# The linear-attention block of a decoder: bias products on 96 rows, a gate by tanh with one reciprocal per head, the residual added on VectorE

## What is computed

```
q, k, v = heads(x @ Wq.T + bq), heads(x @ Wk.T + bk), heads(x @ Wv.T + bv)
g = jax.nn.sigmoid(heads(x @ Wg.T + bg))
q, k = jax.nn.elu(apply_rope(q)) + 1.0, jax.nn.elu(apply_rope(k)) + 1.0
def step(carry, inp):                       # over the two chunks of a sequence
    S, Z = carry
    qi, ki, vi, gi = inp
    S = S + jnp.einsum('bhtd,bhte->bhde', ki, vi)
    Z = Z + ki.sum(axis=2)
    num = jnp.einsum('bhtd,bhde->bhte', qi, S)
    den = jnp.einsum('bhtd,bhd->bht', qi, Z)[..., None] + 1e-06
    return ((S, Z), gi * num / den)
...
x = _layernorm(x + (out @ Wo.T + bo))
```

## Time and profile before

| | |
|---|---|
| median of three runs | 1009.85 us |
| the profiled execution, its own time | 1009.48 us |
| its span, first to last instruction | 1007.7 us |
| mean granted TensorE clock | 0.994 |
| PE busy | 963.4 us (96%) |
| DVE busy | 642.2 us (64%) |
| ACT busy | 444.5 us (44%) |
| POOL busy | 312.0 us (31%) |

### The profile page before, as it was taken

The page is one execution under the profiler, slowest core; times in us unless marked ns, Lnnn a source line. Parts: engine busy times, 40 slices in busy tenths (PEclk is TensorE's granted clock), DMA queues, the critical chain, the costliest instruction groups (busy, mean ns, idle before and its releaser), DMA issues.

```text
span 1007.7 us, 18735 instructions
## 1 busy us (share of the span) xinstructions
PE 963.4 (96%) x6131; PEld 757.6 (75%) x6131; DVE 642.2 (64%) x1466; ACT 444.5 (44%) x870; POOL 312.0 (31%) x514
## 2 busy tenths in 40 slices
PE   7999999999999999999999989998999998999994
PEld 5788886688888888888887745567787775888883
DVE  3776777656555555555557567768777865555555
ACT  4777786422233222323222333325777784333331
POOL 1133123344444444444445130110000106344430
PEclk9999999999999999999999999999999999999998
DMA  8000000255433333333332000011111120554401
GB/s 282 19 17 18 2 2 1 65 169 179 144 127 115 110 112 110 116 110 110 110 113 88 0 10 1 1 34 38 30 33 36 34 67 21 126 154 109 111 20 42
DMA packets 37356, 75.20 MB, mean 75 GB/s; under 512 B 7116, under 2 KB 18360, under 8 KB 37154
## 3 DMA queue, kind: packets, MB, share of 16 engines
q1 hardware_dynamic: 37006, 74.18, 25.5%
q0 software_dynamic: 288, 0.23, 0.2%
HBM read 67.21 MB, written 2.40 MB: 69 GB/s over the span
## 4 chain that ended last, share of the span: by engine, by line
PE 87%; DVE 7%; issue 2%; ACT 1%; POOL 1%; DMA 0%; SPq 0%; POOLq 0%; DVEq 0%; ACTq 0%
PE ps L1053 34%; PE ps L1079 17%; PE ps L424 5%; PE ps L674 3%; PE ps L519 3%; PE ps L431 3%; PE ps L913 2%; PE ps L511 2%; PE ps L550 2%; PE ps L791 1%; PE ps L846 1%; PE ps L841 1%; DVE ps L1748 1%; PE ps L810 1%; PE ps L888 1%
## 5 line engine op out<-in xcount | busy, mean ns | idle before, releaser
L1053 PE MATMUL ps<-shared 128*128 128x512 f32 x1560 | 377.8, 391 | 1.2 <-POOL shared L2096 0.7
L1053 PEld LDWEIGHTS ps<-shared 128*128 128x128 f32 x1560 | 292.9, 188 | 65.4 <-issue 4.9
L1489 ACT ACTIVATE shared<-pT 128x512 fp32r<-128x512 f32 x130 | 82.2, 632 | 286.5 <-DVE pT L1909 286.5
L2109 POOL CAST shared<-wraw 128x512 fp32r<-128x512 f32 (+1 forms) x130 | 92.2, 709 | 293.1 <-PE ps L1079 279.5
L1912 DVE TENSOR_TENSOR al<-pT,shared 128x512 fp32r<-128x512 f32 x130 | 118.8, 914 | 90.8 <-ACT shared L1489 90.8
L1901 DVE TENSOR_TENSOR e<-e,ps 128x512 f32<-128x512 f32 x130 | 89.3, 687 | 122.1 <-PE ps L1053 117.8
L1079 PE MATMUL ps<-shared 128*128 128x512 f32 x520 | 160.3, 389 | 0.4 <-DVE al L1912 0.4
L2111 POOL TENSOR_TENSOR shared<-wraw,shared 128x512 fp32r<-128x512 f32 (+1 forms) x130 | 132.1, 1017 | 10.4
L1079 PEld LDWEIGHTS ps<-shared 128*128 128x128 f32 x520 | 97.5, 188 | 21.4 <-DVE al L1912 1.3
L1483 ACT ACTIVATE e<-ps 128x512 f32<-128x512 f32 x130 | 77.7, 597 | 73.4 <-PE ps L1053 73.4
L1909 DVE TENSOR_TENSOR pT<-e,kbd 128x512 f32<-128x512 f32 x130 | 99.9, 769 | 7.1
(11 more groups left out here) (230 smaller groups left out, 1397.8 us busy)
## 6 DMA issues: line engine op xcount, KB each, us to landing
kbd<-combine_C SPq DMA_DIRECT2D x46, 512.0 KB
wraw<-in_C_w SPq DMA_DIRECT2D x48, 384.0 KB, 8.6
kbd<-combine_F SPq DMA_DIRECT2D x15, 512.0 KB
wraw<-in_F_w SPq DMA_DIRECT2D x17, 384.0 KB, 6.9
kbd<-kbd SPq DMA_DIRECT2D x96, 32.0 KB, 1.9
kT<-kbd SPq DMA_DIRECT2D x48, 32.0 KB, 1.8
c_ctx_t<-in_ctx_t SPq DMA_DIRECT2D x1, 1024.0 KB, 9.1
out<-c_x_rows SPq DMA_DIRECT2D x2, 512.0 KB, 3.0
```

The costliest lines, as they stand in the source:

```text
L1053: mm = pe.matmul(GU[t][s], w[u][:, (c * 2 + s) * P:(c * 2 + s + 1) * P], xx[:, c, t * HALF:(t + 1) * HALF], start=(i == 0), stop=(i == 5))
L1489: act.activation(ah[t][:, :], a2[t], ACT.Copy).then_inc(S("ah"), 1)
L2109: pool.tensor_copy(wh[u][:, lo:hi], wraw[k][:, lo:hi]).then_inc(S("m_wh"), 1)
```

## The change

Four things are changed, all in block D:

1. The bias rows are 96 instead of 33, of which 94 are zeros, in the three kinds of bias product (L672 twice and L725 once per sequence); the DMA and the GpSimd cast of these rows grow with them.
2. The gate is sigmoid(g) = (1 + tanh(g/2)) / 2. `gates` calls Tanh where it called Exp, and `linear_out` takes the reciprocal of 2 (den + 1e-6), 16 numbers per token, and multiplies it by 1 + tanh; before, it took the reciprocal of (1 + exp(-g)) (den + 1e-6), 256 numbers per token.
3. The residual is added by VectorE when it reads the output projection from PSUM; the product with the identity (L726) and ScalarE's `linear_z` go.
4. `numerators` waits for `D_an` first, and for the first two sequences issues three products of `pe_keep_pace` before its other waits.

```diff
-        braw = arena[0:33, filled["DE"]:filled["DE"] + 5 * D + P]
+        braw = arena[0:96, filled["DE"]:filled["DE"] + 5 * D + P]
...
-                    pe.matmul(ps[:, n, :], ones33[:, :], brow[:, n * HALF:(n + 1) * HALF], start=True, stop=False)
+                    pe.matmul(ps[:, n, :], ones96[:, :], brow[:, n * HALF:(n + 1) * HALF], start=True, stop=False)
...
             def numerators(b):
 
+                if b > 0:
+                    pe.wait_ge(S("D_an"), b)
+                if b < 2:
+                    pe_keep_pace(pe, 5, 3)
                 pe.wait_ge(S("D_qf"), b + 1)
                 pe.wait_ge(S("D_gm"), b + 1)
-                if b > 0:
-                    pe.wait_ge(S("D_an"), b)
...
-                pe.matmul(y_, ones33[:, :], brow[:, 2 * HALF:], start=True, stop=False)
-                pe.matmul(y_, ident[:, :], X[:, b, :], start=False, stop=False)
+                pe.matmul(y_, ones96[:, :], brow[:, 2 * HALF:], start=True, stop=False)
...
-                    act.wait_ge(S("D_div"), 3 * (b - 2) + 2)
+                    act.wait_ge(S("D_div"), 3 * (b - 2) + 3)
...
-                act.activation(eg[b % 2][:, :], ps[:, 1, 0:D], ACT.Exp, scale=-1.0).then_inc(S("D_eg"), 1)
+                act.activation(eg[b % 2][:, :], ps[:, 1, 0:D], ACT.Tanh, scale=0.5).then_inc(S("D_eg"), 1)
...
-            def linear_z(b):
-
-                act.wait_ge(S("y"), nb("D", b + 1))
-                if b >= 2:
-                    act.wait_ge(S("xn"), nb("D", b - 1))
-                act.activation(z[b % 2][:, :], ps[:, 6, 0:D], ACT.Copy).then_inc(S("z"), 1)
...
-                dve.tensor_scalar(den2, num[:, :, :, DH0], 1e-6, None, ALU.add).then_inc(S("D_div"), 1)
+                dve.tensor_scalar(den2, num[:, :, :, DH0], 1e-6, 2.0, ALU.add, ALU.mult).then_inc(S("D_div"), 1)
                 dve.wait_ge(S("D_div"), 3 * b + 1)
+                dve.reciprocal(dinv[:, :], den[:, :]).then_inc(S("D_div"), 1)
+                dve.wait_ge(S("D_div"), 3 * b + 2)
                 dve.wait_ge(S("D_eg"), b + 1)
-                dve.scalar_tensor_tensor(d2[:, :].rearrange("p (h w) -> p h w", w=DH0),
+                dve.scalar_tensor_tensor(r2[:, :].rearrange("p (h w) -> p h w", w=DH0),
                                          eg[b % 2][:, :].rearrange("p (h w) -> p h w", w=DH0), 1.0,
-                                         bc(den[:, :], 2, DH0), ALU.add, ALU.mult).then_inc(S("D_div"), 1)
-                dve.wait_ge(S("D_div"), 3 * b + 2)
-                dve.reciprocal(r2[:, :], d2[:, :]).then_inc(S("D_div"), 1)
+                                         bc(dinv[:, :], 2, DH0), ALU.add, ALU.mult).then_inc(S("D_div"), 1)
...
+            def linear_residual(b):
+
+                dve.wait_ge(S("y"), nb("D", b + 1))
+                dve.tensor_tensor(z[b % 2][:, :], ps[:, 6, 0:D], X[:, b, :], ALU.add).then_inc(S("z"), 1)
+                dve_stats(dve, "D", b, b % 2)
...
                 if at(t - 4) is not None:
-                    dve_stats(dve, "D", t - 4, t % 2)
+                    linear_residual(t - 4)
...
-            pool.tensor_copy(rows33, braw[:, :]).then_inc(S("brow"), 1)
+            pool.tensor_copy(rows96, braw[:, :]).then_inc(S("brow"), 1)
...
-    d["D_brow"] = np.zeros((33, 5 * D + P), np.float32)
+    d["D_brow"] = np.zeros((96, 5 * D + P), np.float32)
```

More of the change, by code:

```diff
@@ L162, in build @@
         gm = oT[:, 0, :].rearrange("p (n c k) -> p n c k", n=2, c=C)
-        rows33 = shared[2][0:33, 0:5 * D + P]
-        brow = shared[2][0:33, 0:5 * D]
-        ones33 = shared[2][0:33, 5 * D:5 * D + P]
+        rows96 = shared[2][0:96, 0:5 * D + P]
+        brow = shared[2][0:96, 0:5 * D]
+        ones96 = shared[2][0:96, 5 * D:5 * D + P]
         den = sb("den", [P, 16])
-        d2 = sb("d2", [P, D])
+        dinv = sb("dinv", [P, 16])
         r2 = sb("r2", [P, D])
@@ L1378, in act_linear_cross @@
             for t in range(B + 1):
-                if at(t - 4) is not None:
-                    linear_z(t - 4)
                 if at(t - 3) is not None:
@@ L1400, in act_linear_cross @@
                 ep, es, ev, ef, el = (at(t - B - n) for n in range(5))
-                if t == B + 1:
-                    linear_z(t - 4)
                 for k in range(STEPS):
@@ L1421, in act_linear_cross @@
                         masks(es, k + 1)
-                    if k == 3 and do is not None:
-                        linear_z(do)
                     if k == 3 and ep is not None:
@@ L1677, in linear_out @@
                 num = ps[:, 4:6, 0:D].rearrange("p r (m w) -> p r m w", w=VW)
-                two = [x[:, :].rearrange("p (r m w) -> p r m w", r=2, w=DH0) for x in (eg[b % 2], d2, r2, an)]
+                two = [x[:, :].rearrange("p (r m w) -> p r m w", r=2, w=DH0) for x in (r2, an)]
                 den2 = den[:, :].rearrange("p (r m) -> p r m", r=2)
-                dve.tensor_scalar(den2, num[:, :, :, DH0], 1e-6, None, ALU.add).then_inc(S("D_div"), 1)
+                dve.tensor_scalar(den2, num[:, :, :, DH0], 1e-6, 2.0, ALU.add, ALU.mult).then_inc(S("D_div"), 1)
                 dve.wait_ge(S("D_div"), 3 * b + 1)
+                dve.reciprocal(dinv[:, :], den[:, :]).then_inc(S("D_div"), 1)
+                dve.wait_ge(S("D_div"), 3 * b + 2)
                 dve.wait_ge(S("D_eg"), b + 1)
-                dve.scalar_tensor_tensor(d2[:, :].rearrange("p (h w) -> p h w", w=DH0),
+                dve.scalar_tensor_tensor(r2[:, :].rearrange("p (h w) -> p h w", w=DH0),
                                          eg[b % 2][:, :].rearrange("p (h w) -> p h w", w=DH0), 1.0,
-                                         bc(den[:, :], 2, DH0), ALU.add, ALU.mult).then_inc(S("D_div"), 1)
-                dve.wait_ge(S("D_div"), 3 * b + 2)
-                dve.reciprocal(r2[:, :], d2[:, :]).then_inc(S("D_div"), 1)
+                                         bc(dinv[:, :], 2, DH0), ALU.add, ALU.mult).then_inc(S("D_div"), 1)
                 dve.wait_ge(S("D_div"), 3 * b + 3)
@@ L1690, in linear_out @@
                     dve.wait_ge(S("D_atr"), b)
-                dve.tensor_tensor(two[3], num[:, :, :, 0:DH0], two[2], ALU.mult).then_inc(S("D_an"), 1)
+                dve.tensor_tensor(two[1], num[:, :, :, 0:DH0], two[0], ALU.mult).then_inc(S("D_an"), 1)
+            def linear_residual(b):
+                dve.wait_ge(S("y"), nb("D", b + 1))
+                dve.tensor_tensor(z[b % 2][:, :], ps[:, 6, 0:D], X[:, b, :], ALU.add).then_inc(S("z"), 1)
+                dve_stats(dve, "D", b, b % 2)
             def residual(b):
@@ L1813, in dve_linear_cross @@
                     if k == 4 and do is not None:
-                        dve_stats(dve, "D", do, do % 2)
+                        linear_residual(do)
                     if k == 4 and ep is not None:
```

## The result

The changed kernel took 1002.92 us in the median of five runs (1001.23 to 1003.81). The kernel before, run beside it, now has 1012.53 in the median of its five (1009.58 to 1013.3). The ratio is 0.9912, 95% interval 0.9894 to 0.993: faster by some 9 us, where 12 were forecast, and 0.9 us above the upper end of the range. Profiled execution against profiled execution, it is 1002.89 against 1009.48, or 6.6 us for a sum of 11.95.

The account below looks back on a forecast made before the run. TensorE was taken to bound the middle of block D, VectorE the head of block E. Terms -10.0 - 1.55 + 0.34 - 0.73 = -11.95 us took the profiled 1009.48 to 997.5, 997.9 for the median; range 995.5 to 1002.

Parts of the forecast that it names:

- first sequences: Start of block D: numerators(0) at about 600.85 us instead of 602.72, 1.87 us earlier, with project(0)'s and project(1)'s gains included.
- step 2: Block D's second step, with project's saving only: -0.76 us and half a change of array back, -0.70 us.
- the six steps up to numerators(7): Block D: steps 3 to 7 lose 1.49 us each, -7.45, and linear_project(5) a further 0.73.
- wait for block E's first scores: Head of block E: SyncE's chain of DMA issues sets the first scores, so linear_project(5)'s 0.73 us is lost waiting.
- linear_out(7), addition, linear_project(7): Around block E's head: smaller reciprocal -1.55 us, VectorE's residual addition +0.34, cheaper linear_project(7) -0.73.
- dips of the clock: TensorE's clock fall at 850 to 855 us, absent or doubled in another execution: 1.7 us either way.
- Part 1: Block D's bias products: 33 rows cost 0.38 us each that 96 would not; 0.76 us off per project.
- Part 2: Gate by tanh, 16 reciprocals: 1.55 us less VectorE work per sequence, worth nothing in PE-bound steps, 1.55 us at linear_out(7).
- The drain behind a load: First sequence: some 1.38 us on top of the activation table load would make numerators(0) about 1.4 us later, time 999.3.
- Part 3: Residual on VectorE: linear_project goes from 1.80 to 1.07 us on PE; the addition, some 0.42 us, is hidden in steps.
- The masks: Rival in block D: masks take PE's place, a 0.88 us wait returns in five steps, 4.4 us given back, 1002.3; 11%.
- Slower by the clock: Rival: TensorE's clock falls to 1.2 GHz within block D; lasting through steps 1 to 3, 1019 us; 2%.

Follow-up runs that it names:

- Experiment 1: Kernel before unchanged, 1012.18 us, and with the changed kernel's tile places, 1018.44; changed kernel unchanged, 1004.44, and with the old tile places, 1000.0.
- experiment 2: Changed kernel with holes ahead of al, so that al starts 128, 0 or 96 bytes past a multiple of 256: 1003.42, 999.6 and 1010.41 us.
- experiment 3: Kernel before with only its bias products put on 96 rows, 1006.26 us; changed kernel with them on 64 rows, 1013.03 us; single executions.
- before_again: Kernel before, with no edit, profiled a second time: median 1012.18 us, ratio 0.9998.
- after_al192: Changed kernel with a hole of 192 bytes per partition ahead of al, which then starts at a multiple of 256: median 999.6 us, ratio 0.9855.

## Why the prediction was wrong

**The step that failed** is the first choice of the prediction, to go past blocks C and F because "nothing in them is edited except the loading of the bias rows". The diff does edit them: by one allocation, d2 to dinv, which moves al to a start 64 past a multiple of 256. That costs 4.3 us, and no bound was set for it; without it the measured 1002.92 would be about 998.6, within the range. Experiment 1 shows it from both sides, experiment 2 narrows it to al.

**The sum, term by term**, against the profiled 1009.48:

| term | forecast | measured |
|---|---|---|
| first sequences | -1.87 | -1.71 |
| step 2 | -0.70 | -0.53 (7.58 to 7.05) |
| the six steps up to numerators(7) | -8.18 (-7.45 and linear_project(5)'s -0.73) | -7.94 |
| wait for block E's first scores | +0.73 | +0.92 (3.70 to 4.62) |
| linear_out(7), addition, linear_project(7) (block E's first scores to the 121st) | -1.94 | -2.28 (73.83 to 71.55) |
| blocks C and F: start of al | not costed | +4.3 |
| dips of the clock: 850 gone, 184 new | within +/-1.7 | +0.7 |

The first five rows are -11.5 of -11.95, with errors of either sign up to 0.34 that in part cancel; the largest is the addition's 0.34, which was not on the path. The last is a difference between two executions. The fifth al starts 2.55 us later than before, nearly all of it lost in the dip:

```profile
206.72 0.69 DVE L1906 TENSOR_TENSOR al<-pT,shared 128x512 fp32r<-128x512 f32 x1 [0.70 <-ACT shared L1477]
```

In the kernel before it starts at 204.17. Against that, the 1.7 us of 850 to 855 are not lost again.

**Part 1** was right in mechanism and size, but for L727's 0.10 per step, which the step's 7.65 instead of 7.58 shows. That 96 rows behave as 100 was a choice; experiment 3 bears it out.

**Part 2** was right about the load, which moved. The drain behind a load, by which the time would have been 999.3, is not in the trace: 0.02 us. The reciprocal of 16 takes 253 ns, not 200, hidden. What the prediction missed is that the wide one would have become the bound: it called it worth nothing in the steps.

**Part 3** is in the 7.65. The addition takes 418 ns (forecast 420), hidden.

**The masks**, the likeliest rival, did not take TensorE's place: it waits 0.31 us for them at numerators(0), behind the three products of part 4, and is busy 35.87 of 36 us in the steps:

```profile
612.00:648.00 36.00, 35.87 (x250) 20.93 (x249) 26.54 (x64) 12.45 (x31) 6.90 (x24) 1.00 0.01 1
```

**The first scores** come 4.62 us behind numerators(7), before 3.70. The wait behind SyncE's chain of DMAs takes back 0.92 us, all that the last step gained (8.62 to 7.71); the prediction had 0.73 for both. The last key DMA is issued from 660.53, which is 1.44 us behind numerators(7), where it was 0.53 before:

```profile
660.53 1.84 SPq L383 DMA_DIRECT2D kT<-kbd  x3
```

**Slower by the clock**, the rival for block D, did not happen: from the first L672 to block E's first scores the clock is 1.00 in every profile, with or without the products of part 4. Behind that it dips at 670 to 688 us in five of the fourteen profiles, one of them of the kernel before (before_again). Dips there, at 184 and at 829 to 858 us come and go with the execution. The base of the forecast, 1009.85 from three runs, was a low draw: 17 later runs have 1012.59 in the median. Against that, -11.95 is 1000.6, and the two kernels with al on a multiple of 256 have 1000.0 and 999.6. They are the fastest here, 0.987 and 0.9855 of the kernel before. That the sum comes so near is in part luck, since its terms err both ways.

## What to carry to other kernels

An edit that changes the size of a tile edits every product that reads a tile allocated behind it: compare the start addresses of both builds before calling a block untouched, and give operands of hot products a start on a multiple of 256 bytes, which costs 192 bytes in each partition here (after_al192) and was worth 4.3 us. A bias product on 33 or 64 rows, amid products on all of them, costs 0.2 us itself and 0.2 at its successor; zeros up to 96 rows take both away. When one engine's share of a step is cut, the work hidden under it has to be measured against the new step, not the old.

## What the runs showed of the hardware

- A product of 512 fp32r columns that streams an operand whose start is 64, 96 or 128 bytes past a multiple of 256 slows itself and its successors, with no wait and no clock to show for it (other starts were not tried). The six down products, two of which read al, and the twelve behind them cost 13.3, 33.3 and 66.7 ns more at 128, 64 and 96 bytes past a multiple of 256. At 96 nine distances behind the second product that reads al still show it, at 64 three.
- 33 and 64 rows have the same price to 0.01 us, 96 and 100 have the other.
- A bias product behind `sums`, whose weights have 64 columns, costs 0.31 us whatever its rows (33, 64 or 96); behind full ones 0.12 on 96 and 0.31 on 33 and 64.
- The clock goes to its lower level for some 3 to 7 us in some executions and not in others of the same kernel, always near a change of block (184, 670 to 688, 829 to 858 us). The dip of 3.4 us at 675 makes block E's first 121 scores 1.5 us longer (73.83 to 75.35 in before_again), and the one of 6.8 us at 184 costs about 2.4. The start differs too: VectorE's third maximum starts anywhere from 20.2 to 23.2 us in the fourteen profiles. Of the 17 runs the four over 1015 us have mean granted clocks of 0.985 to 0.987, the others 0.989 to 0.994, so the dips make a good part of the 6.7 us between the fastest and the slowest; no run isolates it.
